# Attention with keys projected once, four head tiles of probabilities, and all denominators from pair sums

## The reference

```python
xq = rope(q @ Wq)                      # 1024 columns: 16 heads x 64
xk = rope(kv @ Wk); xv = kv @ Wv       # 512 columns each; kv = q
xk = jnp.repeat(xk, 2, axis=-1)        # each key column stands twice
xv = jnp.repeat(xv, 2, axis=-1)
scores = softmax(xq @ xk * scale)      # per head, 512 x 512, scale 0.5
out = (scores @ xv) @ Wo
# rope: real = xe*cos - xo*sin, imag = xe*sin + xo*cos, even and odd dims interleaved
```

## Time and profile before

| | before |
|---|---|
| median of three runs | 2701.39 us |
| the profiled execution: its time, its span | 2698.95 us, 2697.2 us |
| attention phase | from about 18 us to about 1,614 us of the span |
| one full iteration (two neighbours, 1010.37 to 1198.12 us) | 93.9 us |
| PE busy in these two | 170.21 of 187.75 us |
| DVE, ACT, POOL busy in these two | 137.60, 116.75, 113.91 us |

### The profile page before, as it was taken

The page is one execution under the profiler, slowest core; times in us unless marked ns, Lnnn a source line. Parts: engine busy times, 40 slices in busy tenths (PEclk is TensorE's granted clock), DMA queues, the critical chain, the costliest instruction groups (busy, mean ns, idle before and its releaser), DMA issues. The chain is left out here.

```text
span 2697.2 us, 38247 instructions
## 1 busy us (share of the span) xinstructions
PE 2181.0 (81%) x12996; PEld 947.5 (35%) x12996; DVE 1910.3 (71%) x4700; ACT 1478.3 (55%) x2794; POOL 1491.9 (55%) x1344
## 2 busy tenths in 40 slices
PE   2689988988898899899889864678778777877477
PEld 1223323332332333233233222444444444444343
DVE  5777777777677677767777522677888788786487
ACT  2166566656656665665666553446556555654155
POOL 3365665656566556656656431365566556655266
PEclk8799999999999999999999976788989898997599
DMA  2212112111211211121112001000000000000021
GB/s 109 51 46 56 32 30 50 36 44 34 54 36 26 50 40 40 38 50 36 26 46 47 6 9 44 4 13 13 9 9 17 9 9 13 13 5 5 20 67 47
DMA packets 73281, 86.81 MB, mean 32 GB/s; under 512 B 9216, under 2 KB 59520, under 8 KB 72960
## 3 DMA queue, kind: packets, MB, share of 16 engines
q1 hardware_dynamic: 73088, 84.37, 12.5%
HBM read 21.16 MB, written 12.58 MB: 13 GB/s over the span
## 5 line engine op out<-in xcount | busy, mean ns | idle before, releaser
L320 DVE TENSOR_REDUCE mS<-ps 128x1 f32<-128x512 f32 x1024 | 677.2, 681 | 304.0 <-PE ps L655 299.3
L452 ACT ACTIVATE pr<-ps 128x512 f32<-128x512 f32 x1024 | 585.7, 597 | 392.8 <-PE ps L639 373.5
L518 POOL TENSOR_TENSOR prs<-pr 128x512 f32<-128x512 f32 x384 | 487.2, 1288 | 248.9 <-ACT pr L452 248.9
L639 PE MATMUL ps<-qst,kst 97*128 97x512 f16 x1024 | 398.5, 392 | 52.7 <-ACT pr L452 51.5
L655 PE MATMUL ps<-kst,qst 96*128 96x512 f16 x1024 | 402.4, 394 | 34.1 <-DVE mS L320 23.3
L677 PE MATMUL ps<-pr,vt 128*32 128x512 f32 x2048 | 282.1, 624 | 0.0
L639 PEld LDWEIGHTS ps<-qst,kst 97*128 97x128 f16 x1024 | 99.2, 98 | 422.2 <-ACT pr L452 306.2
L522 POOL TENSOR_TENSOR terms<-terms 128x512 f32<-128x512 f32 x128 | 162.4, 1269 | 89.2 <-DVE terms L313 89.2
L313 DVE TENSOR_TENSOR terms<-ps,rope 128x512 f32<-128x512 f32 x256 | 173.2, 679 | 34.8 <-POOL lo L527 28.8
L527 POOL TENSOR_TENSOR lo<-terms,hi 128x512 f16<-128x512 f32 x128 | 148.0, 1157 | 76.9 <-ACT hi L432 76.9
L655 PEld LDWEIGHTS ps<-kst,qst 96*128 96x128 f16 x1024 | 101.3, 99 | 147.2 <-DVE mS L320 76.6
(11 more groups left out here) (266 smaller groups left out, 4434.5 us busy)
## 6 DMA issues: line engine op xcount, KB each, us to landing
qst<-hi SPq DMA_DIRECT2D x128, 128.0 KB, 2.4
kst<-hi SPq DMA_DIRECT2D x128, 128.0 KB, 2.4
qst<-lo SPq DMA_DIRECT2D x64, 128.0 KB, 2.4
kst<-lo SPq DMA_DIRECT2D x64, 128.0 KB, 2.4
x<-in_q SPq DMA_DIRECT2D x16, 256.0 KB, 2.9
rope<-in_rope SPq DMA_DIRECT2D x1, 4096.0 KB, 12.8
x<-yold SPq DMA_DIRECT2D x16, 256.0 KB, 2.5
m_x<-x SPq DMA_DIRECT2D x16, 256.0 KB, 2.8
```

Source lines behind the costliest of these rows:

```text
L320: v.tensor_reduce(mS[:, b % 2, t, s:s + 1], ps[:, 2 + n % 2, :], AX, ALU.max).then_inc(S["s_read"], 1)
L452: a.activation(pr[:, s % 2, g, :], ps[:, g % 2, :], ACT.Exp, scale=ATT_SCALE).then_inc(S["exp"], 1)
L518: g.tensor_tensor(prs[:, c, :], pr[:, 0, c, :], pr[:, 1, c, :], ALU.add).then_inc(S["prs"], 1)
L639: mm(ps[:, g % 2, :], kst[:, h, P * kt:P * kt + P], qst[:, h, :], start=True, stop=True).then_inc(S["st"], 1)
```

## The change

Seven things are changed, all in the attention phase and the loads ahead of it.

1. The columns of Wq and Wk are laid out so that a projection of the keys holds only even or only odd dims (`head_dims`, `k_pairs`). Each of the four key projections is made once and read by two products: even times cos and odd times sin give the real half, the same two projections with the tables swapped give the imaginary half. An iteration has 12 projections instead of 16, and 16 products as before; the rope tables shrink from 16 to 12 blocks.
2. The two halves of a key head now lie in different tiles, so `kst` is filled by 12 DMAs of 16 rows a group instead of three of 32.
3. `pr` has room for four head steps instead of two, `prs` for two pairs. Exponentials of a head step wait for the values of the step four back.
4. `add_pair` runs for every odd head step (32 additions an iteration, not 24), `denominators` eight times, and `denominators_directly` is gone.
5. Values stand in fixed slots: those of an even head step seven slots after its first one, those of the odd step nine slots after the same slot. Denominators stand in slots 13, 21, and so on; what is late falls into the next iteration (`due`).
6. `yold` lies in `x8`, and `denT` in `den`.
7. The table is new: raw scores lag by 10 slots, not 5; the output is in slot 14, the whole feed-forward part in slot 28, its square root too, the second norm from 30 to 41, the gate in 42, projections from 43 to 57, products from 44 to 61.

```diff
@@ -71,11 +82,13 @@
 
 ATTENTION_AT = {
 
-    "values": (0, 1, 7, 8), "output": 4, "x2": 4, "stats1": 5, "aggr1": 8, "xn1": 11, "turn1": 16, "evac1": 17,
-    "ffn": 18, "squares": 19, "ffn_b": 22, "squares_b": 22, "sqrt": 25, "resid": 25, "stats2": 27, "aggr2": 29,
-    "xn2": 31, "turn2": 36, "evac2": 35, "gate": 37, "gate_in": 37, "gate_top": 41, "gate_count": 45,
-    "project": (37, 38, 39, 40, 41, 42, 45, 46, 47, 49, 50, 51, 53, 56, 59, 60), "high_lag": 3, "low_lag": 2,
-    "denominators_lag": 3, "maxima": 5,
+    "values": (0, 3, 11, 15), "output": 14, "x2": 14, "stats1": 14, "aggr1": 17, "xn1": 21, "turn1": 26, "evac1": 26,
+    "ffn": 28, "squares": 27, "ffn_b": 28, "squares_b": 28, "sqrt": 28, "resid": 28, "stats2": 30, "aggr2": 31,
+    "xn2": 36, "turn2": 41, "evac2": 40, "gate": 42, "gate_in": 42, "gate_top": 47, "gate_count": 52,
+    "project": (43, 44, 46, 47, 48, 49, 50, 51, 52, 53, 54, 57),
+    "product": (44, 45, 46, 47, 48, 49, 50, 51, 52, 53, 54, 55, 56, 57, 58, 61), "high_lag": 2, "low_lag": 1,
+    "pv": (7, 5), "numerators": 17, "dev1": 18, "dev2": 33, "add_squares": 28, "add_squares_b": 28, "xnl": 41,
+    "denominators": 13, "divide": 25, "maxima": 10,
 }
...
+        pr = sb("pr", [P, 4, NT, SEQ])
         mS = sb("mS", [P, 2, NT, HEADS])
...
+        rotated_at, high_at, low_at = ({q + lag: m // 2 for m, q in enumerate(AT["product"]) if m % 2}
+                                       for lag in (0, AT["high_lag"], AT["low_lag"]))
         assert max(high_at) < SLOTS
+
+        def staged(first, count, step):
+
+            at = {}
+            for n in range(count):
+                at.setdefault((first(n) + step * n) % SLOTS, []).append(((first(n) + step * n) // SLOTS, n))
+            return at
+
+        values_at = staged(lambda s: AT["pv"][s % 2], HEADS, NT)
+        numerators_at = staged(lambda j: AT["numerators"], NG, NG * NT)
+        division_at = staged(lambda j: AT["divide"], NG, NG * NT)
+        denominators_at = staged(lambda n: AT["denominators"], HEADS // 2, 2 * NT)
+
...
+            return [(i - 2 - late, n) for late, n in at.get(q, ()) if is_att(i - late)]
 
         def is_new(i):
...
                     g0 = NG * ring(b, j)
-                    dst, rows = ((qst, (hi, lo, hi)), (kst, (hi, hi, lo)))[kq]
-                    for row, src in enumerate(rows):
-                        sp.dma_start(dst[DH * row:DH * row + DH, g0:g0 + NG, :],
-                                     src[r, kq]).then_inc(S["stacked", ring(b, j)], 16)
+                    if kq == 0:
+                        for row, src in enumerate((hi, lo, hi)):
+                            sp.dma_start(qst[DH * row:DH * row + DH, g0:g0 + NG, :],
+                                         src[r, 0]).then_inc(S["stacked", ring(b, j)], 16)
+                        return
+
+                    for row, src in enumerate((hi, hi, lo)):
+                        for odd in range(2):
+                            for s in range(2):
+                                d, r0 = DH * row + DH // 2 * odd, DH * j + DH // 2 * s
+                                sp.dma_start(kst[d:d + DH // 2, g0 + s:g0 + NG:2, :],
+                                             src[r0:r0 + DH // 2, 1, odd:NG:2]).then_inc(S["stacked", ring(b, j)], 16)
 
                 def group_free(b, j):
...
-                    kq, g = p // NG, p % NG
-                    dve.wait_ge(S["pair"], 4 * NG * b + m + 1)
+                    if p < NG:
+                        n, table = m, NG * c + p
+                    else:
+
+                        a, odd = (p - NG) // 2, p % 2
+                        n, table = 2 * (NG + a) + c, 2 * NG + 2 * (odd ^ c) + a
+                    dve.wait_ge(S["pair"], 3 * NG * b + n + 1)
                     if c == 0 and 2 * NG * b + p >= 2:
                         dve.wait_ge(S["lo"], 2 * NG * b + p - 1)
-                    v.tensor_tensor(terms[:, p % 2, c, :], ps[:, 4 + c, :], w["rope"][:, 2 * kq + c, g, :],
+                    v.tensor_tensor(terms[:, p % 2, c, :], ps[:, 4 + c, :], w["rope"][:, table, :],
                                     ALU.mult).then_inc(S["pair_free"], 1)
 
                 def maximum(m):
...
+                        if is_new(i) and q in AT["product"]:
+                            if i == 0 and q == AT["product"][0]:
                                 dve.wait_ge(S["rope_in"], 16)
-                            product(i, product_at[q])
+                            product(i, AT["product"].index(q))
                         if i == 0 and q in ONES_AT:
                             r = NG * ONES_AT.index(q)
                             v.memset(kst[3 * DH:STK, r:r + NG, :], 1.0).then_inc(S["ones"], 1)
...
-                    if g == 0 and head >= 2:
-                        act.wait_ge(S["pv"], head - 1)
-                    if 2 <= s < HEADS - 2 and s % 2 == 0:
-                        act.wait_ge(S["prs"], NG * ((HEADS // 2 - 2) * b + s // 2 - 1) + g + 1)
-                    if s >= HEADS - 2 and g == 0:
-                        act.wait_ge(S["dd"], NT * b + s + 3 - HEADS)
-                    if s < 2 and b and g == 0:
-                        act.wait_ge(S["dd"], NT * b - 1 + s)
+                    if g == 0 and head >= 4:
+                        act.wait_ge(S["pv"], head - 3)
+                    if head >= 4 and s % 2 == 0:
+                        act.wait_ge(S["prs"], NG * (head // 2 - 2) + g + 1)
                     n = SLOTS * b + NG * s + g
                     act.wait_ge(S["st"], n + 1)
-                    a.activation(pr[:, s % 2, g, :], ps[:, g % 2, :], ACT.Exp,
+                    a.activation(pr[:, s % 4, g, :], ps[:, g % 2, :], ACT.Exp,
                                  scale=ATT_SCALE).then_inc(S["exp"], 1)
 
                 for i in range(ITERATIONS):
...
-                    pairs = (HEADS // 2 - 2) * b + n
+                    pairs = HEADS // 2 * b + n
                     pool.wait_ge(S["exp"], SLOTS * b + NG * (2 * n + 1) + c + 1)
-                    if pairs:
-                        pool.wait_ge(S["dn"], pairs)
-                    g.tensor_tensor(prs[:, c, :], pr[:, 0, c, :], pr[:, 1, c, :], ALU.add).then_inc(S["prs"], 1)
+                    if pairs >= 2:
+                        pool.wait_ge(S["dn"], pairs - 1)
+                    k = 2 * (n % 2)
+                    g.tensor_tensor(prs[:, n % 2, c, :], pr[:, k, c, :], pr[:, k + 1, c, :], ALU.add).then_inc(S["prs"], 1)
 
                 def rotated(b, p):
...
-                        if is_att(i) and 0 < s < HEADS - NT and s % 2:
+                        if is_att(i) and s % 2:
                             add_pair(i - 2, s // 2, c)
...
-                def project(i, p, c):
-                    kq, g = p // NG, p % NG
-                    if c == 0 and p == 0:
+                def project(i, n):
+
+                    p, c = n // 2, n % 2
+                    if n == 0:
                         pe.wait_ge(S["xnl"], i + 1)
                         if is_old(i):
                             pe.wait_ge(S["gate_read"], i - 2)
                     if p:
-                        pe.wait_ge(S["pair_free"], 4 * NG * i + 2 * p - 1 + c)
-                    wt = [w["wq"][:, h, g, c, :] if kq == 0 else w["wk"][:, h, c, P * g:P * g + P] for h in range(2)]
+                        pe.wait_ge(S["pair_free"], 4 * NG * i + (n - 1 if p <= NG else n + 1))
+                    wt = [w["wq"][:, h, p, c, :] if p < NG else w["wk"][:, h, P * (n - 2 * NG):P * (n - 2 * NG) + P]
+                          for h in range(2)]
                     three_passes(ps[:, 4 + c, :], wt, [xnh[:, i % 2], xnl[:, i % 2]]).then_inc(S["pair"], 1)
 
...
-                        ins = mm(ps[DH * g:DH * g + DH, 6, :], vt[:, kt, DH * h:DH * h + DH], pr[:, s % 2, g, :],
+                        ins = mm(ps[DH * g:DH * g + DH, 6, :], vt[:, kt, DH * h:DH * h + DH], pr[:, s % 4, g, :],
                                  start=kt == 0, stop=kt == NT - 1, skip_group_check=True)
                     ins.then_inc(S["pv"], 1)
 
                 def denominators(b, n):
-                    pe.wait_ge(S["prs"], NG * ((HEADS // 2 - 2) * b + n + 1))
+                    pe.wait_ge(S["prs"], NG * (HEADS // 2 * b + n + 1))
                     if n % 2 == 0 and NG * b + n:
                         pe.wait_ge(S["den"], NG * b + n // 2)
                     for g in range(NG):
-                        ins = mm(ps[DH * g:DH * g + DH, 7, :], w["ones"][:, 0:DH], prs[:, g, :],
+                        ins = mm(ps[DH * g:DH * g + DH, 7, :], w["ones"][:, :], prs[:, n % 2, g, :],
```

## The result

Four runs of the changed kernel gave 2723.24 to 2731.11 us, median 2727.41; four runs of the kernel before on the same chip gave 2700.93. The ratio is 1.0101, with a 95% interval of 1.0087 to 1.0114: the change makes the kernel 1% slower. The profiled run took 2730.49 us.

The account below looks back on a forecast made before the run. The prediction took POOL's queue to hold the back. 2698.95 + 20 (14 iterations) - 3 (beside them) = 2716 us, with 2.4 us for the median 2718; range 2640 to 2775, the forecast's own 2706 to 2742.

Parts of the forecast that it names:

- The iteration: One full iteration, front and back together: 96.0 us against 94.6, 1.4 us more, in 14 iterations 20 us.
- Beside the iterations: Shorter loads, DMAs added in iteration 1, fewer maxima, and two last iterations without a rope: together -3 us.
- The front: Slots 0 to 43: 52.0 us of PE's work and 10.9 us of waits, together 62.9 us.
- slot 31: Front: PE's shifted tile waits 4.0 us for exponential 29, behind ACT's square root; bounds 2.7 to 5.
- The clock: Front: PE's granted clock falls to its lower level after the square root's wait, 1.5 us; bounds 0 and 3.7.
- The back: Slots 44 to 63: POOL's full queue holds it, 33.1 us after the first projection against 38.2 before.
- slot 54: Back: projection 10 waits 3.1 us for bank 4, read by product 10, which needs the fourth low half and a maximum.
- slots 60 and 61: Back: PE waits 1.9 us for an exponential behind a cast, 2.4 us for maximum 59 behind product 14.
- the third rival: The clock falls in the back as well: another 3.7 us an iteration, 2770 us; chance 0.15.
- POOL does not hold the back: Rival: waits stay at 13.5 us, 90.1 us an iteration, 4.5 less, with the rest 2636 us; chance 0.28.
- The signs: Traces expected if right: stores 95 to 98 us apart, POOL never idle, waits at projection 10, slot 31 and `kst`, one clock fall.
- The multiply beside POOL: Slot 59: DVE's multiply by the reciprocals might wait for one pair sum, 1.25 us an iteration, 18 us; left out.

Follow-up runs that it names:

- the table edit: Changed kernel with projections 10 and 11 in slots 56 and 57 (not 54 and 57), DVE's count of choices in slot 63 (not 52): 2725.5 us.
- short sums: Changed kernel with POOL's pair sums of pairs 5, 6 and 7 over 32 of 512 columns: 2702.5 us.
- keys twice: Changed kernel with each key projection made twice, 16 projections, every bank read by one product: 2732.4 us.
- three pairs of terms: Changed kernel with room for three pairs of terms instead of two, the third in sq: 2727.8 us.
- the direct denominators: Changed kernel with projections 10 and 11 and count later, root one slot later, hi keys sent first, denominators of pairs 5 and 6 directly from pr: 2669.9 us.
- the third multiply moved: The kernel with the direct denominators, with DVE's multiply of the third head group by its reciprocals in slot 62 instead of 59: 2671.0 us.

## Why the prediction was right, and where it was not

- *The end and the sign.* 2718 us was forecast, 2727.4 measured, inside the forecast's own range of 2706 to 2742.
- *The iteration.* 96.0 us forecast, 95.15 measured. The old one was taken as 94.6 from one iteration where the mean is 94.0, so that the loss of 1.4 us (20 in all) was close to the measured 1.2 (16). That is luck: 96.0 against the mean would have been 28 us in all.
- *Beside the iterations* the sum had -3 us. The profiled executions are 31.5 us apart and their 13 full iterations 14.7, so about 17 us lie there (the medians are 26.5 us apart). This is the mis-sized term. Ahead of the first shifted tile stand 7.4 us of it; iteration 16, which the prediction had 2.2 us shorter, is 4.2 us longer (83.3 against 79.1); and 6.2 us lie behind the last shifted tile, about half of them in the second layer, which was not changed. The first raw tile starts at 79.0 us against 74.8 in the earlier trace rows, and the first shifted tile at 140.1 against 132.7. The prediction counted the DMAs added once, for the first group; but SyncE now takes 7.6 us for each group's keys (5.12 for eight DMAs, 2.50 for four). With three DMAs 5 us of the 7.4 went. Why iteration 16 is longer is open: the table edit, which leaves POOL's work as it is, brings it to 75.8 us.
- *The front.* 62.9 forecast, 62.5 measured. Its waits: slot 31 4.0 against 2.99 (0.8 us of the first table load, 1.28 us long, ran beside POOL's last sum of squares), slot 10 1.7 against 1.29, slots 34 to 36 0.9 against 0.24, slots 41 and 42 1.2 against 1.1. The clock was set at 1.5 us; slots 31 to 33 took 2.8 us more than slots 7 to 9, which hold the same work, at the full clock (6.32 us against 3.50). So the smaller waits and the dearer clock nearly cancelled.
- *The back.* 33.1 forecast and measured, by terms that did not all hold. Slot 52 0.85 against 0.57, slot 54 3.1 against 2.91, slots 60 and 61 4.3 against 1.44. What the last two lack, the clock took in great part: it fell behind slot 54 as in the third rival, projection 10 took 1.25 us instead of 0.65, and slots 55 to 57 took 6.33 us, where their work at the full clock is 1.53 + 0.44 + 1.53 + 0.65 = 4.15. That rival's event came, but its price of 52 us did not, because the back waited less in exchange.
- *"POOL does not hold the back", the gain, 0.28.* It did not come in this kernel, but for two reasons and not one. The prediction held POOL's full queue alone responsible. Its walk through the slots was close up to product 10: it had the fourth low half end 18.7 us after the first projection starts, and it ended after 18.5. What it missed is that this place holds PE as long without the sums (2.82 us in slot 54). The runs showed two holds: POOL's sums, and what stands ahead of the second reader of bank 4. Taking one off leaves the back at 33 us or above (short sums 33.06, keys twice 35.76, table 35.0); taking both off makes it 29.8 in the iterations shown, 30.5 and 31.5 on the mean. The second hold is itself double: DVE's queue (count, two maxima, product 9) and the row up to the fourth low half end 0.24 us apart, and relieving one (count moved, three pairs of terms) left product 10 where it was. No run relieved both without touching the bank or the sums.
- *The signs.* Stores 95 us apart, the wait of 3 us of projection 10, the raw tile waiting for `kst` and POOL without idle time but for the casts came. Two did not: product 10 was not released by the low half, which was ready 0.24 us earlier, and the clock fell twice an iteration, not once.
- *The multiply beside POOL.* It was weighed at 18 us for one multiply in slot 59 and left out of the sum. The multiplies took 673 ns in the changed kernel, in two iterations, against 785 in the earlier trace rows, so it cost DVE nothing there; POOL's low half beside it paid, with 1.51 us where others took 1.16. It came to DVE in other kernels, as told below.

## What to carry to other kernels

When an edit takes a suspected hold away and nothing moves, look for a second hold in the same stretch before acquitting the first: only the pair of edits tells, and here they took 0.3, -1.9 and together 2.9 us off the stretch. Measure the stretch over all iterations and not the whole time alone: two of these edits met their time with a back and a front that did not do what was expected. An operand that is read twice saves its second production but keeps its buffer until the second reader has come through its own engine's queue and has its other operands and its room, so place the next writer by the last of these. Splitting a transfer into four times as many DMAs costs the issuing queue at the start of the kernel, where nothing covers it, and here also a wait of 1.1 us an iteration.

## What the hardware showed

DVE instructions with two operands in SBUF were slowed by POOL, and others were not. The groups by line over two iterations, the one-hot products with three pairs of terms and the count with the direct denominators (count, busy us, mean ns, idle):

```profile
L76 DVE TENSOR_TENSOR onehot<-iota,gif 128x32 f32<-128x32 f32 x4 | 3.8, 994 | 0.0
```

```profile
L79 DVE TENSOR_TENSOR cnt_acc<-cnt_acc,onehot 128x64 f32<-128x64 f32 x2 | 2.3, 1150 | 0.1
```

The same instructions have means of 370 and 224 ns in two iterations of the changed kernel. With the table edit alone, which moves the count from slot 52 to 63, its mean from 220 to 1,560 us of the span is 1154 ns, against 296 in the changed kernel. The products of the rope, with one operand in PSUM, took 0.68 us in all of these. The Trainium skill (SBUF — State Buffer, Who interferes with whom) says that a VectorE instruction with two SBUF inputs contends with a GpSimd instruction that reads SBUF; these rows agree, and they show that moving an instruction of 0.2 us to another slot can cost 0.9 us. With the third multiply moved, the price went from that multiply to the one-hot products and the count behind it. POOL paid in the changed kernel: its low half beside the multiply of slot 59, which began 0.20 us after the multiply, took 1.51 us where others took 1.16.

```profile
1173.77 1.51 POOL L562 TENSOR_TENSOR lo<-terms,hi 128x512 f16<-128x512 f32 x1 [0.73 <-ACT hi L471]
```
